# Local attention and feed-forward of a decoder's second layer: 32 by 64 score tiles, a turned value product with a ones column, windows filled by DMA, and adds moved to GpSimd

## The chip, the cores and the metric

The kernel runs on one NeuronCore of a Trainium2 chip. The metric is device time in microseconds (us) of one execution, the median of several runs. The profile is that of one such execution. Engines are named as in the profile: PE (TensorE), PEld (its weight loads), DVE (VectorE), ACT (ScalarE), POOL (GpSimd) and SP (SyncE, which issues the DMAs here).

## The reference, cut to what matters

The whole program is a four-layer decoder with twelve stages, one after another. The change touches only the stage `l1_ffn`, the feed-forward part of the second layer, which is itself a small transformer of six layers over 4 sequences of 256 tokens with 128 features, all in float32:

```python
def local_attention(q, k, v):          # 16 heads of 64, windows of 32 tokens
    ...
    bk2, bv2 = (look(bk), look(bv))    # keys of the window before and of this one: 64
    mask = (it < jb) | (it > jb + w) | (jb == -1)
    sim = jnp.einsum('bhwie,bhwje->bhwij', bq, bk2) * QK_SCALE
    sim = jnp.where(mask, -jnp.finfo(sim.dtype).max, sim)
    attn = jax.nn.softmax(sim, -1)
    out = jnp.einsum('bhwij,bhwje->bhwie', attn, bv2)
```

Ahead of it q and k are projected from the tokens (half of the features shifted by one token), normalised to unit length per head and rotated with position tables; behind it stand the output projection `Wo`, a residual, a layer norm, a gated GELU feed-forward with 341 inner features, and a second residual. A query thus sees at most 33 keys, all of them within 64.

## The kernel before, in words

A **unit** is one sequence in one of the six layers: 24 units. The heads are taken in pairs, an **item** c of 0 to 7 (features of the two heads j = 0, 1 on partitions 0 to 63 and 64 to 127). A unit's body has eight **slots**; slot k is the part of the plan that holds the scores S of item k. The order of work is written out by hand, one string per engine (`PE_PLAN`, `DVE_PLAN`, `ACT_PLAN`, `POOL_PLAN`, lines 3183 to 3189), and `l1_ffn_run` (line 3275) issues exactly that order. Each engine's queue is in order. A prime after a name means the unit before; projections run one unit ahead of the plan's unit, and the feed-forward steps one behind. Bodies -2 to 1 and the last ones are written out, those between are a loop of five rounds with four bodies each. `after(eng, steps, name, unit)` (line 3161) is a wait on the semaphore of a named step.

The names in the plans: p0 to p11 are projections (128 tokens by 512 columns, line 3516; 0 to 7 queries and keys, 8 to 11 values); q squares them (ACT, 3453); r (DVE, 3358 to 3377) multiplies by the tables (L3367, twice L3370), sums the squares (L3372), adds the two halves for even u (L3375) and clamps the sum (L3377); n (POOL, 3307) adds for odd u (L3310), takes the power -1/2 (L3312) and multiplies (L3314); t turns two item's queries or keys (PE, 3532), and e copies them out (ACT, 3458). S is the score product of an item: two bf16 products that write the band mask into two banks (L3542), then products of 128 queries by 128 and 160 keys for each head (L3546). max is the negated row maximum (DVE, L3382), X the four exponentials with accumulated row sums (ACT, L3472), inv the reciprocal of the sums (DVE, L3387), s the scaling of the weights (POOL, L3320), edge a 32-row transpose for the keys that reach over the tile's border (DVE, L3392), T four transposes of weights (PE, L3568), c their copy out of PSUM (ACT, L3479), V the value product, features by tokens, in three shapes of tile (PE, L3578, L3580, L3583), att its copy out (DVE, L3396). y1 is the output projection (PE, 3591), x1 the residual, mean, var and spread with centre, vareps, root (POOL), diag and xn the layer norm, gate and value the inner products, gelu (ACT, 3488), g the gating (DVE, 3434), y2 (PE, 3640) and x2 the second residual; xs makes the shifted copy for the unit to come.

PSUM has eight banks of 512 float32 columns. Scores alternate between banks 0, 1 and 2, 3; banks 4 and 5 alternate for items, turned tiles and value projections; 6 and 7 serve the projections and the feed-forward steps.

## Time and profile before

| | |
|---|---|
| median of 3 runs | 2709.92 us (2708.59 to 2713.13) |
| span of the profiled execution | 2709.9 us |
| mean granted TensorE clock | 0.927 of 2.4 GHz |
| PE matmuls, share of the span | 2399.8 us, 89% |
| DVE | 1612.7 us, 60% |
| ACT | 1232.8 us, 45% |
| POOL | 1033.8 us, 38% |
| DMA | 42.03 MB, mean 16 GB/s |

The profiled execution's own span and the median of the runs are the same to 0.1 us. Busy shares are means over twelve stages; the stage at hand runs from 754 to 1912.7 us, from the first shifted copy (L3343) to the last turn of the result. Within it the starts of the band products (L3542) mark the slots. In a steady unit they lie, from slot 0 on, 4.55, 7.45, 5.98, 7.47, 5.31, 5.22, 5.28 and 5.31 us apart. A matmul on float32 data shows as two records (two passes) in the trace; starts of records are measured, ends modelled.

### The profile page before, as it was taken

Reading aid. Unit: us, or ns where it says so; the run is one execution under the profiler, and the core shown is the slowest. Engines: PE = TensorE matmul, PEld = TensorE weight load, DVE = VectorE, ACT = ScalarE, POOL = GpSimd, SP = SyncE. Lnnn points to the kernel's source line nnn. Section 1 sums busy time; section 2 is a strip of 40 time slices with the busy share of each in tenths; the row PEclk is TensorE's granted clock in tenths of the full one; section 3 lists DMA queues with packets and bytes.
Section 4 is the critical chain, followed back from the end, with each engine's and each line's share of the span. In section 5 each row is a group of like instructions: output and inputs, shape, how many; then the busy total and the mean of one; then the engine's idle time right before and its main releaser. Section 6 shows DMA issues by size and latency. Waiting matters only on the chain. (4 is left out here: it accounts for less than half of the span.)

```text
span 2709.9 us, 46097 instructions
## 1 busy us (share of the span) xinstructions
PE 2399.8 (89%) x15951; PEld 1422.1 (52%) x16003; DVE 1612.7 (60%) x3811; ACT 1232.8 (45%) x3219; POOL 1033.8 (38%) x901
## 2 busy tenths in 40 slices
...
GB/s 59 26 28 1 1 1 1 16 3 2 2 51 5 21 12 15 17 17 14 13 17 25 9 10 25 9 9 1 12 6 0 31 31 5 19 2 25 24 35 20
DMA packets 45348, 42.03 MB, mean 16 GB/s; under 512 B 7421, under 2 KB 35749, under 8 KB 45108
## 3 DMA queue, kind: packets, MB, share of 16 engines
...
q14 instruction: 104, 0.85, 0.1%
HBM read 33.36 MB, written 0.52 MB: 13 GB/s over the span
## 5 line engine op out<-in xcount | busy, mean ns | idle before, releaser
L3320 POOL TENSOR_TENSOR l1fb_p<-l1fb_p,l1fb_rden 128x640 f32<-128x640 f32 x192 | 240.4, 1252 | 218.7 <-DVE l1fb_rden L3387 218.7
L3312 POOL TENSOR_TENSOR l1fb_rinv<-l1fb_ssq,neghalf 128x8 f32<-128x8 f32 x192 | 319.2, 1662 | 8.5 <-DVE l1fb_ssq L3377 8.4
L3516 PE MATMUL ps<-l1fb_wqkv,l1fb_xs 128*128 128x512 f32 x576 | 298.3, 628 | 9.1 <-DVE l1fb_xs L3343 4.3
L3472 ACT ACTIVATE l1fb_p<-ps,l1fb_shift 128x128 f32<-128x128 f32 (+1 forms) x768 | 281.9, 391 | 0.3
L3314 POOL TENSOR_TENSOR l1fb_qk<-l1fb_qk,l1fb_rinv 128x512 f32<-128x512 f32 x192 | 206.6, 1076 | 15.0
L3479 ACT ACTIVATE l1fb_pT<-ps 128x512 f32<-128x512 f32 x192 | 114.7, 597 | 191.3 <-PE ps L3568 191.3
L3453 ACT ACTIVATE l1fb_sq<-ps 128x512 f32<-128x512 f32 x192 | 114.8, 598 | 170.1 <-PE ps L3516 167.7
L3382 DVE TENSOR_REDUCE l1fb_shift<-ps 128x4 f32<-128x640 f32 x192 | 157.2, 819 | 52.0 <-PE ps L3546 50.0
L3472 ACT ACTIVATION_READ_ACCUMULATOR l1fb_p<-ps,l1fb_shift 128x1 f32 x768 | 167.8, 219 | 0.0
L3568 PE MATMUL ps<-ident,l1fb_p 128*128 128x128 f32 x768 | 125.8, 286 | 39.7 <-ACT l1fb_g L3488 27.3
L3546 PE MATMUL ps<-l1fb_kT,l1fb_qT 64*128 64x128 f32 (+1 forms) x1536 | 147.3, 310 | 0.0
L3370 DVE TENSOR_TENSOR l1fb_r<-ps,l1fb_turn_tab 128x256 f32<-128x256 f32 x384 | 143.2, 415 | 0.0
L3516 PEld LDWEIGHTS ps<-l1fb_wqkv,l1fb_xs 128*128 128x128 f32 x576 | 96.8, 191 | 86.4 <-issue 69.9
L3367 DVE TENSOR_TENSOR l1fb_qk<-ps,l1fb_turn_tab 128x512 f32<-128x512 f32 x192 | 131.9, 687 | 12.0 <-ACT l1fb_sq L3453 9.4
L3372 DVE TENSOR_REDUCE l1fb_ssq<-l1fb_sq 128x8 f32<-128x512 f32 x192 | 129.9, 676 | 0.0
L3546 PEld LDWEIGHTS ps<-l1fb_kT,l1fb_qT 64*128 64x128 f32 x1536 | 100.8, 187 | 50.9 <-issue 50.9
L3532 PE MATMUL ps<-ident,l1fb_qk 128*128 128x128 f32 x768 | 117.6, 276 | 9.3 <-POOL l1fb_qk L3314 6.5
L3310 POOL TENSOR_TENSOR l1fb_qk<-l1fb_qk,l1fb_r 128x512 f32<-128x512 f32 x96 | 122.1, 1271 | 0.0
L3568 PEld LDWEIGHTS ps<-ident,l1fb_p 128*128 128x128 f32 x768 | 80.4, 140 | 75.8 <-ACT l1fb_g L3488 28.7
L475 DVE TENSOR_REDUCE l3x_nm<-ps 128x1 f32<-128x512 f32 x128 | 82.7, 687 | 58.5 <-PE ps L356 58.3
L2828 DVE TENSOR_TENSOR l3f_mid<-ps,l3f_act 128x512 f32<-128x512 f32 x64 | 44.2, 691 | 118.1 <-PE ps L2988 78.2
L447 ACT ACTIVATE l1a_e<-ps 128x512 f32<-128x512 f32 x128 | 69.6, 595 | 95.3 <-PE ps L368 95.2
...
## 6 DMA issues: line engine op xcount, KB each, us to landing
...
```

What stands on the lines that cost most here:

```text
L3310: nc.gpsimd.tensor_tensor(w.qk[:, u, :], w.qk[:, u, :], w.r2[:, 1, :], ALU.add).then_inc(*w.unit_norm.end(f"add{u}"))
L3312: nc.gpsimd.tensor_tensor(w.rinv[:, u, :], w.ssq[:, u, :], chip.neghalf[:, 0:8], ALU.pow).then_inc(*w.unit_norm.end(f"rinv{u}"))
L3314: nc.gpsimd.tensor_tensor(heads(w.qk[:, u, :]), heads(w.qk[:, u, :]), w.rinv[:, u, :].unsqueeze(2).to_broadcast([P, 8, FFN_DH]), ALU.mult) ...
L3320: nc.gpsimd.tensor_tensor(p, p, w.rden[:, c, :, :].rearrange("p j q -> p (j q)").unsqueeze(2).to_broadcast([P, 2 * QT, SEEN]), ALU.mult)\
L3367: nc.vector.tensor_tensor(r1, src, tab(0, slice(0, DH)), ALU.mult)
L3370: last = nc.vector.tensor_tensor(r2[:, :, o], src[:, :, other], tab(1, o), ALU.mult)
L3372: nc.vector.tensor_reduce(w.ssq[:, u, :], heads(w.sq[:, u % 2, :]), AX.X, ALU.add).then_inc(*w.rot.end(f"ssq{u}"))
L3382: nc.vector.tensor_reduce(w.shift[:, c, :, :], ps[:, bank:bank + 2, 0:2 * SEEN].rearrange("p j (q n) -> p j q n", n=SEEN), AX.X, ALU.max, ...
L3472: last = nc.scalar.activation(w.p[:, c % 4, j, q, 0:hi - lo], ps[:, SCORE_BANK(c) + j, lo:hi], ACT.Exp, bias=w.shift[:, c, j, q:q + 1], ac ...
L3516: nc.tensor.matmul(ps[:, PROJ_BANK(u), :], w.xs[:, x.odd, q * P:(q + 1) * P], w.wqkv[:, col:col + 512], start=True, stop=True)\
L3546: last = nc.tensor.matmul(ps[:, bank + j, at:at + n], w.qT[rows, x.odd, c, q * P:(q + 1) * P], w.kT[rows, x.odd, c, key:key + n], start=Fa ...
L3568: last = nc.tensor.transpose(ps[:, ITEM_BANK(c), at:at + P], w.p[:, c % 4, j, q, q * EDGE:q * EDGE + P], chip.ident[:, :])
```

## The change

What it does, part by part. Scores: for each window of 32 queries and each head one product of 32 queries by 64 keys, on a PE tile of 64 rows and 32 columns, 16 products an item in place of 4; the keys get 32 columns of zeros in front, the band has 128 columns in place of 320. The weights of an item are then 128 by 256, and two transposes turn them for both heads. Values: the product is turned round, 16 products of 32 queries by 65 columns (64 features and a column of ones that gives the row sum), from values stored window by window; the odd windows are projected directly (`odd_window`, two tiles side by side), and the even ones are copied from them by four SBUF-to-SBUF DMAs a unit (`even_windows` on SP). The division comes behind the value product (att on DVE, a product in place of a copy), POOL's scaling, the edge transpose and the accumulated sums go, and the result needs two transposes (in T of the next item) and goes with c through ACT. The adds for even u move from DVE to POOL; the clamp becomes a tensor_tensor. Two waits are new in place: G (values_ready) and B (band) stand ahead of V and S. Banks: scores only 0, 1; values, y, mean, var, spread and the two value chunks 2, 3; items 4; turned tiles and value projections 5; projections 6 and 7, with the gates. The weights' buffers go from four to two. Lines of the diff that are left out rename, or change a bank's number in the way just said.

```diff
-HALF_HEADS = ((0, 0), (1, 0), (0, 1), (1, 1), (2, 0), (2, 1))
+HALF_HEADS = ((0, 0), (1, 0), (0, 1), (1, 1))
-SCORE_BANK = lambda c: c % 2 * 2
-ITEM_BANK = lambda c: 4 + c % 2
-PROJ_BANK = lambda u: 6 + u % 2 if u < QK else 4 + (u + 1) % 2
-TURN_BANK = lambda n: 4 + (n + 1) % 2
+SCORE_BANK, VALUE_BANK, ITEM_BANK, TURN_BANK = 0, 2, 4, 5
+PROJ_BANK = lambda u: 6 + u % 2
-PE_PLAN = """S0 T6' t4' gate01' V6' gate2'    S1 T7' t5' p0 value01' V7' value2' p1    S2 T0 t6' y2' V0 p2    S3 T1 t7' y1 V1 p3
-             S4 T2 t0 mean V2 p8 p4           S5 T3 t1 var V3 p9 p5                    S6 T4 t2 V4 p10 p6     S7 T5 t3 spread V5 p11 p7""".split()
-DVE_PLAN = """inv7' att5' max0 edge6' r7' tab    inv0 att6' max1 edge7' g0' g1' r0 g2'  inv1 att7' max2 edge0 x2' r1  inv2 att0 max3 edge1 r2 x1
-              inv3 att1 max4 edge2 centre r3     inv4 att2 max5 edge3 vareps r4          inv5 att3 max6 edge4 diag xs r5  inv6 att4 max7 edge5 xn r6""".split()
-ACT_PLAN = """c6' e4' X0 gelu0' gelu1' gelu2'    c7' e5' q0 X1 q1    c0 e6' X2 q2    c1 e7' X3 q3
-              c2 e0 X4 v8 q4    c3 e1 X5 v9 q5    c4 e2 X6 v10 q6    c5 e3 X7 v11 q7""".split()
-POOL_PLAN = """s7' n6'    s0 n7'    s1 n0    s2 n1    s3 n2    s4 n3 root    s5 n4    s6 n5""".split()
+PE_PLAN = """G6' B0 V6' S0 t4' gate01' T7' gate2'    G7' B1 V7' S1 t5' T0 p0 value01' p1    G0 B2 V0 S2 t6' T1 p2 y2' p8    G1 B3 V1 S3 t7' T2 p3 y1 p9
+             G2 B4 V2 S4 t0 T3 p4 mean p10       G3 B5 V3 S5 t1 T4 p5 var p11          G4 B6 V4 S6 t2 T5 p6          G5 B7 V5 S7 t3 T6 p7 spread""".split()
+DVE_PLAN = """inv6' att6' max0 r7' tab    inv7' att7' max1 g2' r0 g0' g1'    inv0 att0 max2 r1 x2'    inv1 att1 max3 r2 x1
+              inv2 att2 max4 r3 centre    inv3 att3 max5 r4 vareps           inv4 att4 max6 r5 diag xs    inv5 att5 max7 r6 xn""".split()
+ACT_PLAN = """e4' X0 c7' gelu0' gelu1' gelu2'    e5' X1 c0 q0 q1    e6' X2 c1 q2 v8    e7' X3 c2 q3 v9
+              e0 X4 c3 q4 v10    e1 X5 c4 q5 v11    e2 X6 c5 q6    e3 X7 c6 q7""".split()
+POOL_PLAN = """n6'    n7'    n0    n1    n2    n3 root    n4    n5""".split()
...
+            def even_windows(t):
+                sp.wait_ge(*w.vals.done("v11", t))
+                for j in range(2):
+                    v = w.v[DH * j:DH * j + DH, t % 2, :, :, :].rearrange("p w c d -> p w (c d)")
+                    sp.dma_start(v[0:EDGE, 2:WINDOWS:2, :], v[EDGE:DH, 1:WINDOWS - 2:2, :]).then_inc(w.dup_in, 16)
+                    sp.dma_start(v[EDGE:DH, 0:WINDOWS:2, :], v[0:EDGE, 1:WINDOWS:2, :]).then_inc(w.dup_in, 16)
...
+            for k in range(-1, B * L + 1):
+                l = (k + 2) // B
+                if 0 < k < B * L and k % B == 0:
+                    out_weights(k // B)
+                if B < k < B * L and k % B == 1:
+                    feed_weights(k // B)
+                changed = k % B == 2 and l < L
+                if changed:
+                    for n in range(3):
+                        scores_weights(l, n)
+                    value_weights(l)
+                if k + 1 < B * L:
+                    even_windows(k + 1)
+                if changed:
+                    scores_weights(l, 3)
...
     def unit_norm(x, u):
-        if u % 2:
-            after(eng, w.rot, f"rot{u}", x)
-            nc.gpsimd.tensor_tensor(w.qk[:, u, :], w.qk[:, u, :], w.r2[:, 1, :], ALU.add).then_inc(*w.unit_norm.end(f"add{u}"))
+        after(eng, w.rot, f"rot{u}", x)
+        nc.gpsimd.tensor_tensor(w.qk[:, u, :], w.qk[:, u, :], w.r2[:, u % 2, :], ALU.add).then_inc(*w.unit_norm.end(f"add{u}"))
...
-        nc.vector.tensor_scalar(w.ssq[:, u, :], w.ssq[:, u, :], 1e-24, None, ALU.max).then_inc(*w.rot.end(f"clamp{u}"))
+        nc.vector.tensor_tensor(w.ssq[:, u, :], w.ssq[:, u, :], fp(w.tiny), ALU.max).then_inc(*w.rot.end(f"clamp{u}"))
...
     def attended(x, c):
-        after(eng, w.V, f"V{c}", x)
-        nc.vector.tensor_copy(w.attT[:, x.odd, c, :], ps[:, ITEM_BANK(c), 0:S]).then_inc(*w.att.end(f"att{c}"))
+        after(eng, w.T, f"T{(c - 1) % ITEMS}", x.past(0 if c else 1))
+        after(eng, w.inv, f"inv{c}", x)
+        nc.vector.tensor_tensor(w.att[:, c % 2, :, :, :].rearrange("p q j d -> p j q d"), by_head()[:, :, :, 0:DH],
+                                w.rden[:, c % 2, :, :].unsqueeze(3).to_broadcast([P, 2, QT, DH]), ALU.mult).then_inc(*w.att_made.end(f"att{c}"))
...
         for j in range(2):
-            for q, (lo, hi) in enumerate(((0, P), (SEEN, 2 * SEEN))):
-                last = nc.scalar.activation(w.p[:, c % 4, j, q, 0:hi - lo], ps[:, SCORE_BANK(c) + j, lo:hi], ACT.Exp,
-                                            bias=w.shift[:, c, j, q:q + 1], accum_out=w.den[:, c, j, q:q + 1])
+            for q in range(QT):
+                last = nc.scalar.activation(w.p[:, c % 2, q, j, :], ps[:, SCORE_BANK + j, q * SEEN:(q + 1) * SEEN], ACT.Exp, bias=w.shift[:, c, j, q:q + 1])
...
+    def odd_window(x, u):
+        m = u - QK
...
+        weights = w.wqkv[:, 2 * H * DH:3 * H * DH].rearrange("p (c j d) -> p j c d", j=2, d=DH)
+        for j in range(2):
+            last = nc.tensor.matmul(ps[DH * j:DH * j + DH, TURN_BANK, :].rearrange("p (c d) -> p c d", d=DH), w.xs[:, x.odd, SEEN * m:SEEN * m + SEEN],
+                                    weights[:, j, :, :], start=True, stop=True, tile_position=(0, DH * j))
+        last.then_inc(*w.proj.end(f"p{u}"))
...
+    def values_ready(x, c):
+        after(eng, w.kept, f"c{c}", x)
+        if c == 0:
+            eng.wait_ge(w.dup_in, x.t * 64 + 64)
+        after(eng, w.att_made, f"att{(c - 1) % ITEMS}", x.past(0 if c else 1))
+        if c in (0, 1):
+            after(eng, w.norm, ("g1", "x2")[c], x.past(2))
+        elif c in (2, 3, 4, 6):
+            after(eng, w.norm, {2: "x1", 3: "diff", 4: "vareps", 6: "xn0"}[c], x.past(1))
+
+    def band(x, c):
         if c % 2 == 0:
             after(eng, w.turned, f"e{c // 4 * 4 + 2 + c // 2 % 2}", x)
-        after(eng, w.X, f"X{(c - 2) % ITEMS}", x.past(0 if c >= 2 else 1))
+        after(eng, w.X, f"X{(c - 1) % ITEMS}", x.past(0 if c else 1))
...
+    def scores(x, c):
+        for n in range(WINDOWS):
+            q, at = n // 4, EDGE * (n % 4)
             for j in range(2):
                 rows = slice(DH * j, DH * j + DH)
+                last = nc.tensor.matmul(ps[at:at + EDGE, SCORE_BANK + j, q * SEEN:(q + 1) * SEEN], w.qT[rows, x.odd, c, EDGE * n:EDGE * (n + 1)],
+                                        w.kT[rows, x.odd, c, EDGE * n:EDGE * n + SEEN], start=False, stop=(q == 1), tile_position=(DH * j, at))
         last.then_inc(*w.S.end(f"S{c}"))
 
+    def values(x, c):
+        for n in range(WINDOWS):
+            q, at = n // 4, EDGE * (n % 4)
+            for j in range(2):
+                rows = slice(DH * j, DH * j + DH)
+                last = nc.tensor.matmul(ps[at:at + EDGE, VALUE_BANK + j, q * (DH + 1):(q + 1) * (DH + 1)],
+                                        w.both[rows, ITEMS * x.odd + c, 0, EDGE * n:EDGE * (n + 1)],
+                                        w.v[rows, x.odd, n, c, :], start=True, stop=True, tile_position=(DH * j, at))
+        last.then_inc(*w.V.end(f"V{c}"))
```

## Rows read from the trace of the kernel before

**Rows 1.** Windows: length, busy us (instructions) per engine, clock, DMA share, GB/s

```profile
1333.17:1379.74 46.57, 44.41 (x308) 28.14 (x307) 38.04 (x93) 31.25 (x97) 37.09 (x30) 1.00 0.04 13
...
1333.17:1345.17 12.00, 10.76 (x78) 6.83 (x77) 8.81 (x22) 9.75 (x26) 9.57 (x8) 1.00 0.00 1
...
1345.17:1369.15 23.98, 23.39 (x162) 15.34 (x161) 19.49 (x50) 14.05 (x49) 17.32 (x14) 1.00 0.08 23
...
1369.15:1379.74 10.59, 10.25 (x72) 5.98 (x71) 9.73 (x25) 7.45 (x24) 10.20 (x9) 1.00 0.01 2
...
754.00:1912.70 1158.70, 1080.63 (x7344) 678.87 (x7344) 922.12 (x2226) 746.85 (x2325) 891.59 (x696) 0.99 0.05 15
```

**Rows 2.** Timeline, PE, slot 1: start, us, instruction, [idle before, releaser]

```profile
1340.09 0.66 PE L3568 MATMUL ps<-ident,l1fb_p 128*128 128x128 f32 x4 [1.24 <-ACT l1fb_g L3488]
```

**Rows 3.** Timeline, PE, values and projections of slot 5, scores of slot 6

```profile
1319.78 0.44 PE L3578 MATMUL ps<-l1fb_pT,l1fb_v 128*64 128x128 f32 x4
1320.15 0.30 PE L3580 MATMUL ps<-l1fb_pE,l1fb_v 32*64 32x32 f32 x4
1320.38 0.44 PE L3583 MATMUL ps<-l1fb_pT,l1fb_v 128*64 128x128 f32 x4
1320.75 1.98 PE L3516 MATMUL ps<-l1fb_wqkv,l1fb_xs 128*128 128x512 f32 x4
1322.57 0.43 PE L3542 MATMUL ps<-l1f_band,ident_b 128*128 128x320 bf16 x2
1322.94 0.77 PE L3546 MATMUL ps<-l1fb_kT,l1fb_qT 64*128 64x128 f32 x8
```

**Rows 4.** Timeline, PE, four 32-row tiles in another stage

```profile
2447.24 0.48 PE L368 MATMUL ps<-l3x_q,l3x_k 32*128 32x256 f32 x1
...
2447.26 0.48 PE L356 MATMUL ps<-l3x_k,l3x_q 32*128 32x256 f32 x1
...
2447.56 0.37 PE L368 MATMUL ps<-l3x_q,l3x_k 32*128 32x256 f32 x1
```

**Rows 5.** Groups by line and shape, 1000 to 1700 us: busy, mean ns | idle before

```profile
L3312 POOL TENSOR_TENSOR l1fb_rinv<-l1fb_ssq,neghalf 128x8 f32<-128x8 f32 x119 | 197.9, 1663 | 0.0
...
L3314 POOL TENSOR_TENSOR l1fb_qk<-l1fb_qk,l1fb_rinv 128x512 f32<-128x512 f32 x119 | 127.6, 1073 | 9.3
...
L3382 DVE TENSOR_REDUCE l1fb_shift<-ps 128x4 f32<-128x640 f32 x118 | 96.6, 819 | 31.2 <-PE ps L3546 29.9
...
L3472 ACT ACTIVATE l1fb_p<-ps,l1fb_shift 128x128 f32<-128x128 f32 x238 | 89.2, 375 | 0.2
...
L3370 DVE TENSOR_TENSOR l1fb_r<-ps,l1fb_turn_tab 128x256 f32<-128x256 f32 x238 | 88.7, 415 | 0.0
...
L3367 DVE TENSOR_TENSOR l1fb_qk<-ps,l1fb_turn_tab 128x512 f32<-128x512 f32 x119 | 81.7, 686 | 1.5
...
L3372 DVE TENSOR_REDUCE l1fb_ssq<-l1fb_sq 128x8 f32<-128x512 f32 x119 | 80.5, 676 | 0.0
...
L3310 POOL TENSOR_TENSOR l1fb_qk<-l1fb_qk,l1fb_r 128x512 f32<-128x512 f32 x60 | 76.3, 1272 | 0.0
...
L3453 ACT ACTIVATE l1fb_sq<-ps 128x512 f32<-128x512 f32 x118 | 70.6, 598 | 95.5 <-PE ps L3516 94.1 <-DVE l1fb_ssq L3372 1.4
...
L3377 DVE TENSOR_SCALAR l1fb_ssq<-l1fb_ssq 128x8 f32<-128x8 f32 x119 | 41.2, 346 | 2.0
...
L3392 DVE STREAM_TRANSPOSE l1fb_pE<-l1fb_p 32x64 f32<-32x64 f32 x118 | 28.1, 238 | 3.7
...
L3488 ACT ACT_TABLE_LOAD x15 | 19.2, 1283 | 0.3
...
L3434 DVE SCALAR_TENSOR_TENSOR l1fb_g<-ps,l1fb_col,l1fb_g 128x256 f32<-128x256 f32 x30 | 13.1, 480 | 40.9 <-PE ps L3632 40.9
```

**Rows 6.** Windows around the one fall of the clock within the loop

```profile
1614.84:1618.25 3.41, 1.90 (x15) 1.06 (x14) 1.48 (x5) 0.67 (x2) 0.60 (x2) 1.00 0.04 10
1618.25:1621.66 3.41, 3.10 (x12) 2.22 (x12) 3.31 (x8) 2.48 (x10) 3.33 (x3) 0.50 0.02 5
```

More of the change, by code:

```diff
@@ L3016 @@
 EDGE = 32
-SEEN = P + EDGE
+SEEN = 2 * EDGE
+WINDOWS = S // EDGE
 def l1_ffn_constants():
@@ L3222, in l1_ffn_layers @@
-        w.gate2 = Steps(sem("gate2"), ["gate2"])
+        w.feed = Steps(sem("feed"), ["y1", "mean", "var", "spread", "gate01", "gate2", "value01", "y2"])
         w.xsteps = Steps(sem("xsteps"), ["xs"])
-        w.rot = Steps(sem("rot"), [f"{s}{u}" for u in range(QK) for s in (("rot", "ssq", "clamp") if u % 2 else ("rot", "ssq", "add", "clamp"))])
+        w.rot = Steps(sem("rot"), [f"{s}{u}" for u in range(QK) for s in ("rot", "ssq", "clamp")])
         w.max, w.inv = lasting(chip, "maxima", each("max", ITEMS)), lasting(chip, "inverses", each("inv", ITEMS))
-        w.edge, w.att = Steps(sem("edge"), each("edge", ITEMS)), lasting(chip, "attended", each("att", ITEMS))
@@ L3231, in l1_ffn_layers @@
-        w.scaled, w.root = Steps(sem("scaled"), each("s", ITEMS)), Steps(sem("root"), ["root"])
+        w.unit_norm, w.root = Steps(sem("unit_norm"), [f"{s}{u}" for u in range(QK) for s in ("add", "rinv", "qk")]), Steps(sem("root"), ["root"])
         a = chip.a
@@ L3448, in l1_ffn_act @@
     DH, ps = FFN_DH, chip.ps
+    eng.wait_ge(w.ready, 2)
     def square(x, u):
```

294 lines of the change are left out of this document (134 added, 160 removed).

## The prediction, made before the changed kernel had run

> **What bounds the kernel now.** I read first the busy time per engine in windows, then PE's order of time within one slot, then the groups by line and shape. The change touches one stage, 1158.70 us of the span; it is 24 units, and a steady one takes 46.57 us, of which PE is busy 44.41, DVE 38.04, POOL 37.09 and ACT 31.25 [rows 1]. PE is therefore the bound, with DVE and POOL close behind. The 2.2 us that PE is idle are mostly two waits in slots 0 to 2: 1.24 us for the last GELU [rows 2], 0.59 us in slots 2 to 5 [rows 1]. Everything else is PE's own work, and what the change takes from PE counts in full until another chain ends later.
>
> **PE, score and value tiles.** One item now costs 0.97 us for values (1319.78 to 1320.75, three shapes of tile, so a drain of about 0.1 us behind each), 0.37 us for the two band products (1322.57 to 1322.94) and about 0.7 us for scores: 2.04 us [rows 3]. After: a projection of 512 columns takes 1.82 us for four passes, so 0.85 ns a column and pass [rows 3]. A score product is two passes of 64 columns, 0.055 us each. 16 products stand on 8 tiles, four passes a tile, 0.22 us if all eight run side by side; values the same with 65 columns. With 0.03 for the first load, 0.05 for staggered starts, 0.1 for the drain, both together take 0.62 us, the bands with 128 columns in place of 320 take 0.2: 0.83 us. That eight tiles run at once is in no row. Four tiles do: four first passes start within 0.02 us and the second passes 0.32 us later, load and one pass of 256 columns [rows 4]. The other end is the shortest tiles of this stage, four passes in 0.23 us with their drain [rows 3]: 64 passes would be 3.7 us. I take 0.83, since the rows with the same mechanism are the four tiles; 3.7 stays a rival. Saving 1.2 us an item, 9.7 us a unit.
>
> The Trainium skill (TensorE: Matmul & The Clock Gate, on the 56 ns gap) says that starts of matmuls never come closer than about 25 ns; by it the 64 passes would take 1.6 us instead of 0.52. Rows 4, with 7 ns from tile to tile, disagree for four tiles; no row has eight.
>
> **PE, the rest.** Values are projected in two 64-column tiles of 512 columns: 0.86 as now, plus a load and two changes of shape, 1.1 us, four times: +1.0 us. Transposes stay eight and four per slot (two of weights, two of the divided result), the feed-forward products stay. PE's work falls from 44.4 to about 35.7 us.
>
> **The other engines.** DVE: the maximum reads 256 columns in place of 640. From 676 ns at 512 and 819 at 640 it would be 0.39 us, -0.43 an item; the edge transpose goes, -0.24; four adds of 512 columns go to POOL, some 0.69 each (as L3367's size); the division is one product of 256 columns (L3370, 0.415) where a copy stood; the clamp, 0.35 on average, has 0.17 as its undisturbed size [rows 5]. 38.0 - 3.4 - 1.9 - 2.8 - 1.4 = 28.5 us. POOL: the scaling goes, four adds come: 8 x (1.27 + 1.66 + 1.07) + 0.7 = 32.7 us [rows 5]. ACT: four exponentials of 64 columns without their accumulator reads, about 0.9 us in place of 1.5 (0.375 is the 128-column one [rows 5]): 26 us. The four SBUF copies a unit wait for the last value eviction in slot 5 and are needed at slot 2 of the next body, four slots and over 16 us later, with the DMA engines 0.04 busy [rows 1]: hidden. On SP they stand behind weight loads whose waits end in the same order of slots, so they hold up nothing. If that cover went, PE would wait at V0 of every unit.
>
> **What is late next.** By sums the bound would be PE at 36 us. But two banks became single, and the new order ties the engines into one cycle. Time it from the end of S6, item by item:
> A. DVE, slots 6 and 7, which hold diag, xs and xn: now 9.73 us of DVE work [rows 1]; less two maxima 0.86, two edges 0.48, one add 0.69 leaves 7.7. Then inv6', att6' (0.17 + 0.42) and max0 (0.39): 8.65 us. PE has only about 5.5 us of work there, so DVE sets the pace.
> B. ACT: X0 0.9, c7' 0.6, table load 1.28, three GELUs 1.2, e5' 0.6, table load 1.28, X1 0.9, c0 0.6, q0 0.6 [rows 5], less overlap: 7.7 us. c0 and q0 stand behind X1.
> C. DVE: r0 (0.69 + 2 x 0.42 + 0.68 + 0.17, overlapped 2.05), then g0' and g1' (0.48 each [rows 5]): 3.0 us. The new wait G0 stands at the head of slot 2 on PE and needs g1'. Behind it are queued B2, V0, S2, t6', T1, p2 and y2', so all of PE stops.
> D. PE, slots 2 to 5: 23.98 [rows 1] - 4 x 1.21 - 0.59 of waits + two more projections 1.72 + 1.0 for the four tiled ones = 21.2; then B6, V4, S6, 0.9: 22.1 us.
> Sum 41.45 us a unit. At G0 PE has nothing queued, and 34 short instructions follow; between nothing and some 3 us (the 3.7 above less 0.62) I take 0.5, nearest the four tiles.
>
> **The clock.** Between p1 and G0 PE stands idle for about 4 us. The GELUs end at 8.65 + 0.9 + 0.6 + 1.28 + 1.2 = 12.6 us, less overlap 12.5, g2' at 13.1, and value01' and p1, 0.86 each (two and one products of PE), are through by 15.2; G0 is free at 8.65 + 7.7 + 3.0 = 19.35. In the trace a stretch with PE busy 1.90 of 3.41 us was followed by 3.41 us at a granted clock of 0.50, that is 1.2 in place of 2.4 GHz [rows 6]. An idle time of 4 us should bring such a fall in each unit, and the busy stretch behind it, slots 2 and 3, then starts at 1.2 GHz. Bounds: nothing, or half clock all the way from S6 to G0 (below, +5.3 us). I take about 4 us at half clock, 2.0 us lost. **Unit: 44.0 us**, 2.6 less than 46.57. Between the first and last unit's start lie 23 such steps: 23 x 2.6 = 60 us. Fill, drain and the turns of the loop I leave as they are, at nothing. The profiled execution's span is 2709.9 us and the median of the runs 2709.92, so the sum goes against either: 2650 us.
>
> **Rivals.**
> 1. The clock does not fall, or only briefly: 42.0 us a unit, 2605 us. For it: the unit now has 1.24 us idle in one piece without a fall [rows 2, 6]. Against it: the piece is three times as long. Chance 0.20.
> 2. The cycle is looser than I read it, and the engines' sums set the pace: 35.7 x 46.57 / 44.41 = 37 us, 2490 us. Against it: the order on DVE (r0 ahead of g0', g1') and ACT (c0 ahead of q0) is written out. Chance 0.10.
> 3. Slower: with tiles this short and PE waiting in slots 6, 7, 0 and 1, the clock stays at 1.2 GHz from S6 to G0. PE's 13 us of work there double, S7, spread, gates, T7' and t5' come late, and A to C grow from 19.3 to about 24.6 us: 49.3 us a unit, 2773 us. For it: PE is busy there only 13 of 19 us. Against it: with doubled work PE is hardly idle, which brings the clock back. It decides the sign once half of that stretch runs slow. Chance 0.16.
> 4. Issue or tiles: eight tiles don't run side by side. With V and S at 1.7 us (a third of the way from 0.62 to 3.7), the five PE-bound slots add 5.4 us and the idle time shrinks: about 47.5 us, 2730 us; at 3.7 us the unit passes 58 and the kernel 2950 us. By the 25 ns of the Trainium skill named above it would be the former. Chance 0.09.
> That the change doesn't do what it says is no rival here: the shapes are in the diff.
>
> **Numbers.** Forecast 0.45, rivals as given. Rival 2, the far end of rival 4 and part of rival 3 are left out of the range, which also takes the forecast's own terms (clock 0 to 4 us, burst 0 to 3 us): 2550 to 2760 us. Faster by over 0.2% (about what a measurement of this kernel tells from no change): 0.40 of the forecast's 0.45, and rivals 1 and 2, 0.70; within 0.2%, 0.05; slower 0.25, with rivals 3 and 4.
>
> **What would show it.** Right: a unit of 43 to 45 us; V and S of an item within 0.6 to 0.7 us; a PE wait of about 4 us at V0 or the band of slot 2, ended by DVE's g; granted clock below 1 right behind it; POOL waiting for DVE rather than the other way. Wrong: V with S over 1.2 us (rival 4); clock near 0.5 in slots 6 to 1 (rival 3); no wait before slot 2 and PE over 90% busy (rival 2); PE waiting for a DMA at V0.

## The result, and the profile after

The changed kernel takes **2756.54 us** (median of 4 runs, 2754.95 to 2758.95), the kernel before 2711.53 us on the same chip: ratio 1.0164, 95% interval 1.015 to 1.0178. It is 45 us slower, where 60 us less was forecast. The profiled execution has a span of 2753.8 us against 2709.9, a mean granted clock of 0.895 against 0.927, and 62410 instructions against 46097.

The loss lies in the stage changed. From the first to the last unit's first band product it now takes 1114.3 us (775.28 to 1889.57) against 1068.8: 45.5 us more. A steady unit takes 48.0 to 48.3 us instead of 46.57. The windows of one unit, then of its slots 0, 1, 2 and 7, in the changed kernel:

```profile
core 0: us, PE busy (x) PEld busy (x) DVE busy (x) ACT busy (x) POOL busy (x), PEclk, DMA share, GB/s
1350.58:1398.57 47.99, 38.93 (x666) 25.32 (x667) 34.01 (x80) 25.53 (x65) 32.53 (x26) 0.93 0.13 33
1350.58:1354.67 4.09, 3.89 (x82) 3.01 (x83) 3.47 (x9) 2.38 (x7) 3.22 (x3) 1.00 0.02 6
1354.67:1364.15 9.48, 4.80 (x84) 3.05 (x82) 5.27 (x12) 6.17 (x13) 5.16 (x5) 0.89 0.01 2
1364.15:1371.34 7.19, 7.19 (x87) 4.67 (x87) 4.03 (x9) 2.50 (x7) 5.37 (x5) 0.68 0.00 0
1391.85:1398.57 6.72, 3.61 (x78) 2.30 (x79) 6.50 (x14) 2.88 (x8) 6.45 (x6) 1.00 0.40 95
```

Against [rows 1], PE's busy time has fallen by 5.5 us although part of it ran at half clock, ACT's by 5.7 and POOL's by 4.6: PE's saving is there. But PE is now idle for 9 us of a unit, in slots 1 and 7 above all. DVE, for which 28.5 us was forecast, is at 34.01.

**Tiles.** PE's order of time at the head of slot 0, with the moment the next instruction starts:

```profile
start us, us, engine line op out<-in xcount [idle before <-releaser]
1350.58 0.28 PE L3581 MATMUL ps<-l1f_band,ident_b 128*128 128x128 bf16 x2 [1.42 <-DVE l1fb_diff L3444]
1350.79 0.46 PE L3597 MATMUL ps<-l1fb_v,l1fb_both 64*32 64x65 f32 x32
1351.06 0.59 PE L3588 MATMUL ps<-l1fb_kT,l1fb_qT 64*32 64x64 f32 x32
1351.58 0.66 PE L3562 MATMUL ps<-ident,l1fb_qk 128*128 128x128 f32 x4
```

Bands, values and scores of an item take 1.00 us (1350.58 to 1351.58) against 2.04 before [rows 3] and 0.83 forecast. The 32 passes of V are through within 0.27 us. At the prediction's 0.85 ns a column one after another would take 1.8 us, and the four passes that one of eight tiles has take 0.22, so eight tiles do stand side by side.

**The two waits.** What PE waited for in the stage, and the place where the first of them arises (columns of the second fence as above):

```profile
engine line waited for: us in total, times, longest us
PE ps L3581 <- DVE l1fb_g L3453: 96.8, 21, 5.0
PE ps L3612 <- DVE l1fb_att L3414: 38.0, 25, 2.0
```

```profile
1360.51 0.69 DVE L3391 TENSOR_TENSOR l1fb_qk<-ps,l1fb_turn_tab 128x512 f32<-128x512 f32 x1 [3.31 <-ACT l1fb_sq L3473]
...
1361.95 1.26 POOL L3340 TENSOR_TENSOR l1fb_qk<-l1fb_qk,l1fb_r 128x512 f32<-128x512 f32 x1 [4.04 <-DVE l1fb_r L3394]
1362.49 0.74 DVE L3398 TENSOR_TENSOR l1fb_ssq<-l1fb_ssq,l1fb_tiny 128x8 f32<-128x8 f32 x1
1363.15 0.86 DVE L3453 SCALAR_TENSOR_TENSOR l1fb_g<-ps,l1fb_col,l1fb_g 128x256 f32<-128x256 f32 x2
...
1364.15 0.39 PE L3581 MATMUL ps<-l1f_band,ident_b 128*128 128x128 bf16 x2 [4.68 <-DVE l1fb_g L3453]
```

G0 waits 4.68 us for g1', as forecast (about 4). In the same rows stands what was not: the clamp, a maximum over 128x8, takes 0.74 us and ends at 1363.23, just behind GpSimd's add, which ends at 1363.21. The same in slot 7. There the clamp stands for a multiplication of GpSimd, which ends at 1392.47, and a copy behind it stands for an add, which ends at 1393.95:

```profile
1391.43 1.04 POOL L3344 TENSOR_TENSOR l1fb_qk<-l1fb_qk,l1fb_rinv 128x512 f32<-128x512 f32 x1
...
1391.85 0.65 DVE L3398 TENSOR_TENSOR l1fb_ssq<-l1fb_ssq,l1fb_tiny 128x8 f32<-128x8 f32 x1
...
1392.43 1.52 POOL L3340 TENSOR_TENSOR l1fb_qk<-l1fb_qk,l1fb_r 128x512 f32<-128x512 f32 x1
1392.76 1.35 DVE L3367 COPY l1fb_xs<-l1f_xr 64x256 f32<-64x256 f32 x1
...
1395.21 0.44 PE L3612 MATMUL ps<-ident,l1fb_p 128*128 128x128 f32 x2 [1.70 <-DVE l1fb_att L3414]
```

The copy into xs, 0.28 us in the kernel before, takes 1.35 us; inv5, att5 and max7 come behind it, and T6 on PE waits 1.70 us for att5. DVE's groups over the stage show how regular this is:

```profile
line engine op names shapes xcount | busy us, mean ns | idle before us <-releasers
L3398 DVE TENSOR_TENSOR l1fb_ssq<-l1fb_ssq,l1fb_tiny 128x8 f32<-128x8 f32 x185 | 125.7, 680 | 6.4
L3396 DVE TENSOR_REDUCE l1fb_ssq<-l1fb_sq 128x8 f32<-128x512 f32 x185 | 125.1, 676 | 0.0
L3367 DVE COPY l1fb_xs<-l1f_xr 64x256 f32<-64x256 f32 x22 | 28.6, 1300 | 0.0
```

A clamp of 8 numbers costs as much as a sum over 512, and about twice its mean before (0.346 us in L3377 of [rows 5]). The reduction, which also reads from SBUF alone, is at its old 676 ns. Of the 192 clamps 142 begin while GpSimd is in an add and 27 while it is in a multiplication; the other 23 take 0.17 us.

No list of waits shows this, since the wait lies inside the length of DVE's instruction. The list has POOL waiting for DVE instead (L3340 for L3394, 295 us in the stage), which the prediction had named as a sign of being right.

**The turn of the loop.** The unit with the turn takes 49.2 us and the one behind it 52.4, 5.5 us more than two steady ones; before it was 2.1 to 2.5. The loop has five rounds and so jumps back four times. PE there:

```profile
1447.76 0.28 PE L3581 MATMUL ps<-l1f_band,ident_b 128*128 128x128 bf16 x2 [1.05 <-DVE l1fb_diff L3446]
1447.97 0.46 PE L3597 MATMUL ps<-l1fb_v,l1fb_both 64*32 64x65 f32 x32
1448.24 0.38 PE L3588 MATMUL ps<-l1fb_kT,l1fb_qT 64*32 64x64 f32 x7
1450.37 0.43 PE L3588 MATMUL ps<-l1fb_kT,l1fb_qT 64*32 64x64 f32 x25 [1.75 <-issue]
```

In the middle of S0, behind 7 of its 32 passes, PE stops for 1.75 us for nothing that the profile shows. The same stop stands at each of the four turns, 1.75 to 2.03 us. PE's branch itself takes 3.3 to 3.6 us in the trace, as before. The clock falls there as well: slot 7 of this turn takes 8.01 us at a granted clock of 0.79 (6.72 at 1.00 in a steady unit), the slot 0 behind it 7.34 at 0.77 (4.09 at 1.00). In the kernel before both stay at 1.00.

### The profile page after: what moved, and what is told of

Same layout as the page of the kernel before. It is cut to its first block and busy times, and to the rows that moved or that the text cites. A ratio compares the mean times of both kernels' runs of the same rounds, so it can differ in the third digit from the quotient of the medians.

```text
span 2753.8 us, 62410 instructions
## 1 busy us (share of the span) xinstructions
PE 2283.4 (83%) x24591; PEld 1362.7 (49%) x24643; DVE 1519.4 (55%) x3524; ACT 1097.8 (40%) x2452; POOL 923.2 (34%) x807
## 5 line engine op out<-in xcount | busy, mean ns | idle before, releaser
L3340 POOL TENSOR_TENSOR l1fb_qk<-l1fb_qk,l1fb_r 128x512 f32<-128x512 f32 x192 | 249.4, 1299 | 302.2 <-DVE l1fb_r L3394 300.7
L3530 PE MATMUL ps<-l1fb_wqkv,l1fb_xs 128*128 128x512 f32 x384 | 223.3, 668 | 4.8 <-DMA l1fb_wqkv<-in_L_ffn_Wqkv 4.2
L3493 ACT ACTIVATE l1fb_p<-ps,l1fb_shift 128x64 f32<-128x64 f32 x768 | 177.7, 320 | 44.7 <-DVE l1fb_shift L3404 44.4
L3581 PE MATMUL ps<-l1f_band,ident_b 128*128 128x128 bf16 x384 | 56.7, 232 | 158.9 <-DVE l1fb_g L3453 96.8
L3394 DVE TENSOR_TENSOR l1fb_r<-ps,l1fb_turn_tab 128x256 f32<-128x256 f32 x384 | 143.3, 415 | 0.0
L3479 ACT ACTIVATE l1fb_kT<-ps 128x512 f32<-128x512 f32 x96 | 57.4, 598 | 209.4 <-PE ps L3562 209.4
L3398 DVE TENSOR_TENSOR l1fb_ssq<-l1fb_ssq,l1fb_tiny 128x8 f32<-128x8 f32 x192 | 131.2, 683 | 6.6
L3588 PE MATMUL ps<-l1fb_kT,l1fb_qT 64*32 64x64 f32 x6144 | 118.6, 236 | 7.4 <-issue 7.3
L3501 ACT ACTIVATE l1fb_both<-ps 128x512 f32<-128x512 f32 (+1 forms) x193 | 119.0, 617 | 9.6 <-PE ps L3612 9.6
L3479 ACT ACTIVATE l1fb_qT<-ps 128x512 f32<-128x512 f32 x96 | 57.3, 596 | 142.2 <-PE ps L3562 142.2
L3485 ACT ACTIVATE l1fb_v<-ps 128x512 f32<-128x512 f32 x96 | 57.4, 598 | 137.4 <-PE ps L3545 137.0
```

Source lines behind the costliest of these rows:

```text
L3340: nc.gpsimd.tensor_tensor(w.qk[:, u, :], w.qk[:, u, :], w.r2[:, u % 2, :], ALU.add).then_inc(*w.unit_norm.end(f"add{u}"))
L3394: last = nc.vector.tensor_tensor(r2[:, :, o], src[:, :, other], tab(1, o), ALU.mult)
L3398: nc.vector.tensor_tensor(w.ssq[:, u, :], w.ssq[:, u, :], fp(w.tiny), ALU.max).then_inc(*w.rot.end(f"clamp{u}"))
L3493: last = nc.scalar.activation(w.p[:, c % 2, q, j, :], ps[:, SCORE_BANK + j, q * SEEN:(q + 1) * SEEN], ACT.Exp, bias=w.shift[:, c, j, q:q + 1])
L3501: nc.scalar.activation(w.both[:, ITEMS * x.odd + c, parts, :], ps[:, ITEM_BANK, :].rearrange("p (k t) -> p k t", k=2)[:, parts, :], ACT.Copy)\
L3530: nc.tensor.matmul(ps[:, PROJ_BANK(u), :], w.xs[:, x.odd, q * P:(q + 1) * P], w.wqkv[:, col:col + 512], start=True, stop=True)\
```

## The experiments

Theory W: the time is lost where G0 waits for g1', queued behind r0. Theory P: DVE's instructions stand for GpSimd's. Rival S: a plain sum of busy times. All ratios are to the kernel before; the changed kernel has 1.0164. What a run gained is its median against 2756.54 us. Slot times are those of a steady unit in each profile.

**1. g0' and g1' ahead of r0.**

```diff
-... max1 g2' r0 g0' g1' ...
+... max1 g2' g0' g1' r0 ...
```

> The changed kernel with one place of VectorE's order altered: in slot 1 g0' and g1' stand ahead of r0. Theory W (the wait of G0 for g1', queued on VectorE behind r0, is where slots 1 and 2 lose their time): value01' ends near 1359.1 in the unit from 1350.58, so g0' and g1' take .86 us from there and G0 can issue near 1360.1 instead of 1364.15; TensorE's idle time of 4.7 us falls to about 1; the granted clock of slot 2 (.68) comes back to 1 for the most part; r0 waits for its square until 1360.5 anyway and starts no later. T1 then waits for att0 behind r0 for some 1.5 us. Slots 1 and 2 together go from 16.7 us to 11.5 to 13, the unit from 48.0 to 43 or 44.5, the run to 2640 to 2680 us. Rival P (the time is set by the waits of VectorE's instructions for GpSimd's): the wait moves to T1 and later slots, and less than 1.5 us per unit is gained: 2720 to 2757 us.

Measured 2709.62 us, ratio 0.999 (0.9972 to 1.0007): 47 us gained, less than W's 76 to 116 and more than P's 37 at most. Slot 1 went from 9.48 to 5.8 us. Slot 2 got no shorter: 7.4 us in some units, 8.6 to 10.6 in others, where T1 waits 1.8 us for att0 behind r0, and the clock falls there in some units and not in others. Windows of one unit of each kind:

```profile
1139.10:1183.58 44.48, 37.22 (x666) 23.90 (x667) 34.40 (x80) 25.55 (x65) 32.48 (x26) 1.00 0.14 35
1326.12:1373.80 47.68, 41.34 (x666) 26.23 (x667) 34.59 (x80) 25.77 (x65) 33.02 (x26) 0.89 0.14 33
```

W holds for the place of the wait; about half of what it should give was eaten by the next wait and by the clock.

**2. The price of the clock.** Four matmuls on constants in the wait of G0.

```diff
+        if c == 0:
+            after(eng, w.turned, "e5", x)
+            for _ in range(4):
+                nc.tensor.matmul(ps[:, TURN_BANK, :], chip.ident[:, :], fp(f.xpos), start=True, stop=True)
```

> The changed kernel with four more matmuls of 128x512 on constants ahead of G0 in slot 2, into the bank of the turns that is free there: 3.4 us of work at full clock in a wait of 4.7. It measures what the fall of TensorE's clock costs. Theory C (the half clock behind the wait costs time): granted clock 1.0 through slots 1 and 2, slot 2 5.0 to 5.6 us instead of 7.1 to 7.5, unit 46.0 to 46.5, run 2705 to 2720 us. Rival (slot 2 is paced by VectorE, and the clock costs nothing): slot 2 over 6.8 us at full clock, run 2745 to 2760 us.

Measured 2726.76 us, ratio 1.0046 (1.0027 to 1.0064): 30 us gained by adding work.

```profile
1341.29:1387.40 46.11, 40.50 (x675) 25.43 (x675) 33.92 (x80) 25.42 (x65) 32.52 (x26) 1.00 0.14 34
1354.87:1360.19 5.32, 5.32 (x87) 3.25 (x87) 3.96 (x9) 2.39 (x7) 3.89 (x4) 1.00 0.00 0
```

Slot 2 is 5.32 us at clock 1.00 where it was 7.19 at 0.68: the fall costs 1.9 us a unit. The forecast had 2.0. The run came out 7 us above what was expected: the clock falls in slot 7, at three of the four turns (9.6 to 10.0 us, against 8.0 to 8.3 in the changed kernel) and in seven other units (7.2 to 7.6 us at 0.77, against 6.72 at 1.00).

**3. The even adds back on DVE.**

```diff
+        if u % 2 == 0:
+            nc.vector.tensor_tensor(r1, r1, r2, ALU.add)
```

> The changed kernel with the adds of the even projections back on VectorE, as before. Rival S (a plain sum of busy times: GpSimd's adds relieve VectorE): VectorE gains four adds of .68 to .80 and loses nothing, 37 us, slots 7 and 1 get .7 to .8 us longer each: 2780 to 2800 us.

Measured 2729.58 us, ratio 1.0061 (1.0044 to 1.0078): 27 us faster than with all adds on GpSimd, and S wanted 24 to 44 slower. DVE around slot 7:

```profile
1375.69 0.28 DVE L3368 COPY l1fb_xs<-l1f_xr 64x256 f32<-64x256 f32 x1
...
1379.12 0.68 DVE L3401 TENSOR_TENSOR l1fb_qk<-l1fb_qk,l1fb_r 128x512 f32<-128x512 f32 x1
1379.72 0.16 DVE L3403 TENSOR_TENSOR l1fb_ssq<-l1fb_ssq,l1fb_tiny 128x8 f32<-128x8 f32 x1
```

An even clamp is down to 0.16 us, and the copy of xs to 0.28, no add of GpSimd being under way there. Slot 7 takes 5.80 us instead of 6.72, while slot 2, at a clock of 0.62, takes 7.78 instead of 7.19. DVE's unit is 33.39 us against 34.01: with four adds more it is busy for less. **Moving these adds to GpSimd relieved DVE of nothing**; beside the other parts of the change this one cost 27 us.

**4. The clamp left out** (the maximum with 1e-24 is not computed).

> The changed kernel with the clamp of the sums of squares left out (the maximum with 1e-24 is not computed; GpSimd's power waits for the sum itself). Theory P: each clamp is .17 us of work and .51 of waiting for GpSimd's add; VectorE's busy time of a unit falls from 34.0 by 8 x .68 less what the next instruction with all its operands in SBUF inherits (xs, xn0 reads PSUM): by 4 to 5.5 us; slot 7 (6.7 us) gets 0.5 to 1.2 shorter, slot 1 (9.48) .7: unit 46 to 47, run 2705 to 2735 us. Rival W alone (only g1' behind r0 matters): slot 1 gets .7 us shorter through r0's clamp and nothing else changes: 2735 to 2745 us. Rival S: the clamp costs its own .17 us: 8 x .17 = 1.4 at most, of which slot 1 sees .17: 2750 us.

Measured 2693.44 us, ratio 0.9925 (0.9908 to 0.9943): 63 us gained, 12 beyond P's better end, and faster than the kernel before. DVE's unit falls to 29.39 us, slots 1, 2, 4 and 7 get 0.8, 0.4 to 0.7, 0.5 and 1.1 us shorter. P had left out slot 4 and the clock.

**5. The clamp in its old form.**

```diff
-        nc.vector.tensor_tensor(w.ssq[:, u, :], w.ssq[:, u, :], fp(w.tiny), ALU.max)
+        nc.vector.tensor_scalar(w.ssq[:, u, :], w.ssq[:, u, :], 1e-24, None, ALU.max)
```

> The changed kernel with the clamp in its old form, tensor_scalar with a constant. Theory P (it is the wait for GpSimd's add, whatever the form): each clamp still ends with the add, .66 to .78 us, run 2750 to 2762 us. Rival K (the new form with two operands from SBUF is slow, the old one is not): .17 to .2 us each, run 2695 to 2710 us as without the clamp.

Measured 2753.71 us, ratio 1.0153 (1.0131 to 1.0175): no difference.

**6. GpSimd's adds left out.**

> The changed kernel with GpSimd's adds left out (the second product of the rotation is computed and not added, so the queries and keys are not the reference's). Theory P: the clamps take .16 to .17 us except where a multiplication runs, the copy of xs .28 to .3; slots 1, 4 and 7 as with the clamp left out and the copies moved, 1.3 us less of GpSimd in each projection: unit 43.5 to 45, run 2645 to 2680 us. Rival K: clamps stay at .68 or more and the run is over 2735 us.

Measured 2669.43 us, ratio 0.984 (0.9818 to 0.9861). The clamp's row in runs 5 and 6:

```profile
L3398 DVE TENSOR_SCALAR l1fb_ssq<-l1fb_ssq 128x8 f32<-128x8 f32 x185 | 126.3, 683 | 6.3
```

```profile
L3396 DVE TENSOR_TENSOR l1fb_ssq<-l1fb_ssq,l1fb_tiny 128x8 f32<-128x8 f32 x186 | 31.8, 171 | 6.4
L3366 DVE COPY l1fb_xs<-l1f_xr 64x256 f32<-64x256 f32 x22 | 6.3, 287 | 0.0
```

Both forms take 0.68 us beside the adds, and the new form takes 0.17 without them: the add is the cause, the form is not. P is shown, rival K is out. A steady unit of run 6, with every clamp and copy in its place and only the adds gone:

```profile
1304.30:1348.75 44.45, 38.50 (x667) 25.11 (x667) 28.98 (x80) 25.36 (x65) 22.20 (x18) 0.96 0.14 35
```

**7. The copies of xs behind max7.**

```diff
-... diag xs    inv5 att5 max7 r6 xn
+... diag    inv5 att5 max7 xs r6 xn
```

> The changed kernel with the two copies into xs moved from ahead of inv5 to behind max7 in VectorE's order. Theory P (the first copy takes 1.30 us instead of .28 since it stands for GpSimd's add of r5; where GpSimd is in its power it does not): the copy takes .28 to .3 us, max7 comes 1.3 to 1.6 us earlier, slot 7 goes from 6.7 to 5.6 or 5.9 us, nothing else moves: 2729 to 2738 us. Rival (the wait moves to the next instruction and slot 7 stays bound by VectorE's sum): under .4 us per unit, 2747 to 2757 us.

Measured 2726.58 us, ratio 1.0055 (1.0038 to 1.0072), 30 us gained, 2 to 11 more than expected: slot 7 is 5.36 us. The copy takes 0.40 on average, as an add sometimes still runs.

**8. Both waits out**: no clamp, and the copies behind max7.

> The changed kernel without the clamp (the maximum with 1e-24 is left out) and with the copies into xs behind max7. Theory P (these two waits are what lies between the forecast unit of 44.0 and the measured one): slot 7 4.6 to 5.0 us (5.65 without the clamp alone), the unit 44.2 to 44.8, run 2665 to 2678 us. Rival (something else holds slot 7): slot 7 5.3 us or more, 2685 to 2695 us.

Measured 2674.14 us, ratio 0.9863 (0.9832 to 0.9893).

```profile
1310.70:1355.24 44.54, 38.38 (x667) 25.10 (x667) 29.05 (x72) 25.56 (x65) 32.42 (x26) 0.96 0.14 35
```

The unit is 44.4 to 44.7 us, slot 7 4.77. This is close to the forecast's unit of 44.0, with its wait for g1' and its fall of the clock still in it. The run also saves the clamp's own 0.17 us, and not all waits are out: diag takes 0.81 us in place of 0.41 and the tensor_scalar of xn 1.36 in place of 0.41, each ended 0.15 to 0.28 us behind an instruction of GpSimd. Run 6 saves nothing of DVE's own work, only GpSimd's adds, and comes to the same unit, 44.45 us. So most of what lies between the forecast and the changed kernel's 48.1 us is DVE waiting for GpSimd.

**9. The DMA copies left out** (the even windows of the values hold ones).

> The changed kernel without the DMA copies that fill the even windows of the values, and without G0's wait for them (the even windows then hold ones: their products are not the reference's). Theory H (the copies are hidden in a steady unit, as predicted; they matter at the turn of the loop alone, where they and the reload of the value weights share the DMA engines with TensorE's instructions): steady slots unchanged within .1 us each, units at the turn (49.2 and 52.4 us) up to 3 us shorter in all, run 2738 to 2757 us. Rival D (the copies are on G0's path or delay others): slot 2 or the slots 4, 6 and 7 in which the copies run get shorter by .3 us or more each: 2700 to 2738 us.

Measured 2760.45 us, ratio 1.017 (1.0149 to 1.0191), 3 us above H's range and no gain. Steady slots are the same within 0.02 us, and the turn as well (49.4 and 52.3 us). The copies are hidden, and they are not what makes the turn long.

**10. The even adds on GpSimd in the kernel before**, that part of the change alone.

> The kernel before with one part of the change alone: the adds of the even projections on GpSimd. Theory P: VectorE loses four adds of .80 us of the unit, and four more clamps wait for an add of GpSimd (.17 to .75), xs too; GpSimd goes from 37.1 to 42.1 us of a unit of 46.6, close to full, and its item chain (the scaling of p, on which T waits) comes later behind the adds: 2715 to 2800 us. Rival S: VectorE's time falls by 3.2 us per unit beside TensorE's 44.4 us, which sets the unit: 2705 to 2715 us, no change.

Measured 2714.98 us, ratio 1.0007 (0.9995 to 1.0019): no change, on the border of the two expectations.

```profile
1332.90:1379.21 46.31, 44.67 (x308) 28.11 (x307) 36.27 (x88) 31.30 (x97) 41.84 (x33) 1.00 0.04 13
```

DVE's unit falls by 1.8 us, not 3.2, and POOL's rises by 4.8 to 41.84 of 46.31. Where PE sets the time, as there, a DVE instruction that stands longer costs nothing.

**11 and 12. The loop written out**, in the changed kernel and in the one before.

```diff
-    with eng.Fori(0, rounds) as j:
-        for k in range(2, 2 + B):
-            body(Unit(j, k))
+    for k in range(-2, units + 2):
+        body(Unit(None, k))
```

> The changed kernel with the loop over the middle 20 units written out, so that no engine branches. In the changed kernel a unit whose last slot holds TensorE's branch takes 49.2 us, the one after it 52.4, against 48.1: 5.4 us a turn, five turns. Theory F (the branch of 3.3 us and the pause of 1.9 us within S0 behind it are waits for TensorE's instructions after the jump): both go, the units stay at 48.0 to 48.3 throughout, 27 us less: 2725 to 2735 us. Rival I (the change's larger number of instructions on TensorE, 64 for S and V of an item, is too much for the supply of instructions anywhere, not at the jump alone): pauses of 1 to 2 us in S or V turn up in other places as well, 2740 us or more.

Measured 2751.98 us, ratio 1.0145 (1.0124 to 1.0165): 5 us, not 27. The 27 counted five turns; there are four, 22 us. The turns are gone, and so is any pause within the loop's S or V, but the units are not the steady ones: from the ninth to the twentieth they alternate between 50.5 and 48.5 us.

```profile
1300.01:1348.57 48.56, 40.05 (x667) 25.64 (x667) 34.91 (x86) 25.63 (x65) 32.76 (x26) 0.90 0.10 23
1348.57:1399.00 50.43, 41.09 (x666) 26.80 (x667) 33.95 (x80) 25.63 (x65) 32.27 (x26) 0.89 0.12 31
1348.57:1353.85 5.28, 5.28 (x83) 4.13 (x84) 3.78 (x9) 2.07 (x7) 3.68 (x4) 0.63 0.01 3
```

Slot 0 of every second unit now runs at 0.63, behind slot 7's idle time: one more fall of the clock, worth 1.2 us there. A pair of such units takes 2.8 us more than two steady ones, six times: 17 of the 22 us. How much of the 2.8 beyond these 1.2 follows from the fall is not shown. Rival I, in whose range the time lies, has no support: there is no pause within S or V. F is right on the turns and misses what came with them. Why the fall comes in one arrangement and not in the other is not settled.

> The kernel before with its loop written out in the same way. Its turns cost 1.7 us in the slot of the branch and .4 in the one behind: 2.1 to 2.2 us, five times. Theory F: 10 to 11 us less, 2698 to 2704 us; the turn costs the changed kernel 3.3 us more than this one each time. Rival I: no difference, or slower: 2709 us or more.

Measured 2705.63 us, ratio 0.9969 (0.9958 to 0.998): 7 to 8 us, with units of 46.5 to 46.6 from the third on. Expected were 10 to 11, for five turns; four of 2.1 to 2.5 are 8 to 10.

**13. Four edits together.** g0' and g1' first and r0 behind max2; y2' ahead of p2; xs behind max7; and the clamp as an addition on GpSimd, which keeps it off DVE.

```diff
-... max1 g2' r0 g0' g1'    inv0 att0 max2 r1 ...
+... max1 g2' g0' g1'    inv0 att0 max2 r0 r1 ...
-... S2 t6' T1 p2 y2' p8 ...
+... S2 t6' T1 y2' p2 p8 ...
-        nc.vector.tensor_tensor(w.ssq[:, u, :], w.ssq[:, u, :], fp(w.tiny), ALU.max)
+        nc.gpsimd.tensor_tensor(w.ssq[:, u, :], w.ssq[:, u, :], fp(w.tiny), ALU.add)
```

> The changed kernel with four edits: g0' and g1' ahead of r0, which now stands behind max2; y2' ahead of p2 on TensorE; the copies of xs behind max7; the clamp as an addition of 1e-24 on GpSimd in place of a maximum on VectorE. Theory (both causes at once: the queue order around g1', and VectorE's instructions standing for GpSimd's adds): slot 1 5.8 us as with the order alone, slot 2 5.3 to 6.3 (no half clock, T1 no more behind r0), slot 4 4.5, slot 7 4.3 to 4.8 with the copies of xs at .3 each; unit 40.5 to 42, run 2560 to 2610 us. Rival (one of the two causes is all there is, or GpSimd's longer chain now sets the time): 2640 us or more.

Measured **2611.73 us, ratio 0.963** (0.9609 to 0.965), 2 us above the expected range.

```profile
1285.18:1326.12 40.94, 37.07 (x667) 23.92 (x667) 28.54 (x72) 25.36 (x65) 34.09 (x34) 1.00 0.16 38
1289.27:1295.02 5.75, 4.79 (x83) 3.05 (x82) 2.29 (x6) 5.71 (x13) 4.47 (x5) 1.00 0.01 3
1295.02:1301.09 6.07, 5.39 (x86) 3.26 (x87) 5.03 (x12) 3.54 (x9) 2.81 (x3) 1.00 0.00 0
```

The steady units take 40.9 and 41.9 us in turn, at full clock, slots 1 and 2 together 11.8 instead of 16.7, slot 7 5.00 (4.3 to 4.8 expected). Both causes are real and both count. What y2' ahead of p2 and r0 behind max2 give by themselves has no run.

**14. The same with the even adds on DVE.**

> The run with four edits, and the adds of the even projections back on VectorE. Theory: with the clamps and the copies out of the way of GpSimd's adds, where an add is done hardly matters any more: four adds of .68 to .80 us on VectorE against five us less on GpSimd, in slots that TensorE fills; within 15 us of the other on either side. Rival (VectorE is near its bound in slots 2 and 7): 15 to 40 us slower than with all adds on GpSimd.

Measured 2643.9 us, ratio 0.9746 (0.9728 to 0.9765), 32 us slower: the rival's figure. With the clamps and most of the copies' wait out of the way, the adds do relieve DVE (units of 42.4 to 44.0 against 40.9 to 41.9 us, slot 2 6.8 against 6.07). The theory's "hardly matters" was wrong.

**15. The value weights loaded after the turn.**

> The run with four edits, and the reload of the value weights (512 KB, which falls into the slots of the branch) put behind the start of the next layer's p0. Theory D (TensorE's wait for its instructions at the turn is long because the weights fill the DMA engines then): slots 7 and 0 at the turn, 7.1 and 7.3 us against 5.0 and 4.1, get shorter by 1 us or more together, 5 us of the run or more: 2598 to 2606 us. Rival (the wait is the jump's own): less than .5 us a turn: 2609 to 2615 us.

Measured 2612.75 us, ratio 0.9629 (0.9606 to 0.9651), as without it. The load is not why PE stands at the turn.

**16. The four edits and the loop written out.**

> The run with four edits, with the loop written out. Theory F: units of 40.9 to 41.9 us throughout instead of 43.4 and 44.6 at a turn: 5 x 6.2 = 31 us less, 2575 to 2585 us. Rival I: pauses elsewhere, since the faster unit takes its instructions in quicker: 2600 us or more.

Measured **2583.75 us, ratio 0.9525** (0.9507 to 0.9544), 28 us less and in the expected range; units of 40.7 to 42.7 us. The sum behind the range was off: there are four turns of 5.3 us, not five of 6.2, and the rest comes from units that are a little shorter. It beats the kernel before by 129 us, that kernel with its own loop written out (run 12) by 122, and the changed one by 173.

## Why the prediction was wrong

The cycle through A, B, C and D was the right one, but two terms in it were mis-sized and one cost outside it was taken at nothing. Its terms in the changed kernel (unit from 1350.58; S6 ends at 1389.13, max0 at 1352.42 and 48 us on, r0 starts at 1360.51):

| term | forecast | measured |
|---|---|---|
| A, end of S6 to end of max0 | 8.65 | 11.3 |
| B, to r0 | 7.7 | 8.1 |
| C, to G0 | 3.0 | 3.6 |
| D, slots 2 to 5 to the end of S6, with burst and clock | 22.1 + 0.5 + 2.0 | 25.0 |
| unit | 44.0 | 48.0 |

- **Score and value tiles: right.** 1.00 us an item instead of 0.83, the saving 1.04 instead of 1.2. V and S take 0.79 us, over the 0.6 to 0.7 named as a sign of being right and well under rival 4's 1.2, so rival 4 is out. At full clock PE's unit is 37.07 us (run 13) against 35.7 forecast; 0.17 us eight times is the size of the difference. One reading was slightly off: 1.82 us for four passes of 512 columns [rows 3] is 0.89 ns a column, not 0.85; that changes 0.22 us to 0.23. On the Trainium skill's rule (TensorE: Matmul & The Clock Gate, on the 56 ns gap) that starts are never closer than about 25 ns: 32 passes in 0.27 us are 8 ns apart, and the trace disagrees with it for products that go to eight tiles.
- **G0's wait: right** in place, cause and size (4.68 us, about 4 forecast), and so was the clock behind it (1.9 us by run 2, 2.0 forecast). Rival 1 is out, and so is rival 2, since the order on DVE does hold PE up. Rival 3 is out for the steady unit, where slots 7 and 0 run at 1.00 and slot 1 at 0.89; a piece of it shows at the turns and in run 11.
- **DMA copies: right.** Run 9.
- **The step that failed** is DVE's and POOL's part: "four adds of 512 columns go to POOL" and "the clamp, 0.35 on average, has 0.17 as its undisturbed size". Rows 5 give the mean alone; 0.17 is the median of the 91 clamps of that trace that meet no instruction of GpSimd. I took it although the mean was twice that, and did not ask what made it 0.35: 53 of the 192 clamps in the kernel before already stood for one of POOL's multiplications, 0.86 us each, and the change puts about six of a unit's eight beside an add and one beside a multiplication. Measured: 0.68 each on average, 4.1 us of a unit, and 1.0 for the copy of xs. DVE's 34.01 us is the forecast's 28.5 with these two terms, but for 0.4. They stand in A, where DVE sets the pace (two clamps and the copy, 2.1 of its 2.65 us), in C (r0's clamp, 0.57) and in D, which the forecast took as PE-bound (slot 4, 4.94 us against 4.46 in runs 4 and 6). Run 8 takes them out and lands at 44.4 to 44.7 us and 2674 us; run 6, without the adds, at 44.45 and 2669.
- **Taken at nothing, wrongly: the turn of the loop.** 5.5 us each instead of 2.1 to 2.5, four times: 13 us.
- The sum: 23 x 4.1 = 94 us, and 13 for the turns, less some 3 us in the first and last units, which are shorter, gives 104 of the 105 us between -60 and +45. The clamps and the copy alone are 2.1 + 0.57 + 0.48 = 3.2 us of a unit, 73 us of the run: priced, they turn the 60 us of gain into a small loss.
- That 2756.5 us still lies in the stated range of 2550 to 2760 is luck. The range reached so far for the clock and for the burst of short products, and neither is what went wrong.

The Trainium skill (SBUF — State Buffer, Who interferes with whom) states the rule that I did not weigh: VectorE and GpSimd share one pair of ports; a VectorE instruction with two inputs in SBUF, or a copy or tensor_scalar in a two-port mode, waits in full while a GpSimd instruction holds the pair, and a reduction does not. By it the clamp would have ended behind the add, and the trace agrees: 0.74 us, ended 0.02 us behind the add, the reduction unmoved at 676 ns. The wait goes the other way too: POOL's add at 1392.43, which begins while DVE's diag (two inputs in SBUF) is under way, takes 1.52 us in place of 1.27, 22 times in the stage. In one point the trace differs. GpSimd's power holds nothing up:

```profile
1398.19 1.65 POOL L3342 TENSOR_TENSOR l1fb_rinv<-l1fb_ssq,neghalf 128x8 f32<-128x8 f32 x1
1398.48 0.41 DVE L3446 TENSOR_SCALAR l1fb_diff<-l1fb_diff,l1fb_col 128x256 f32<-128x256 f32 x1
```

The same tensor_scalar beside an add, in run 7, takes 0.99:

```profile
1381.18 1.27 POOL L3340 TENSOR_TENSOR l1fb_qk<-l1fb_qk,l1fb_r 128x512 f32<-128x512 f32 x1
1381.62 0.99 DVE L3446 TENSOR_SCALAR l1fb_diff<-l1fb_diff,l1fb_col 128x256 f32<-128x256 f32 x1
```

Undisturbed it takes 0.41 too. In the kernel before 26 clamps began beside the power and took 0.17 us, and 47 of DVE's adds took 0.68. That makes 13 of POOL's 32.5 us of a unit harmless, and is why it was enough to put xs where an add has almost ended and the power follows.

On the turn, the Trainium skill (Runtime: NRT & Kernel Launch, Instruction fetch mechanics) says that instructions are fetched ahead in sequence and a taken branch breaks that. Runs 11, 12 and 16 agree that the turn's own stop goes when the loop is written out; in 11 and 16 the second goes too. That the second stop, inside S0, is the fetch that 64 short instructions in 0.8 us outrun is only argued, since they go together with the branch. Nor is it shown what lets the clock fall at the turn.
